# Second layer's dense pass: four normalisations issued one at a time, one per projection, in place of one block

## The reference

```python
    x = _layernorm(x + _L0_attn_ref(x, ...), axis=-1)
    x = _layernorm(x + _L0_ffn_ref(x, ...), axis=-1)      # the norm that the change moves
    x = _layernorm(x + _L1_attn_ref(x, ...), axis=-1)     # its q, k, v projections are the dense pass
    x = _layernorm(x + _L1_ffn_ref(x, ...), axis=-1)

    def _L1_attn_ref(x, q_w, q_b, kv_w, kv_b, o_w):
        q = (x @ q_w.T + q_b) * scale
        kv = x @ kv_w.T + kv_b
        k, v = (kv[..., :E], kv[..., E:])
        q = _rope(q)
        k = _rope(k)
        ...
```

## Time and profile before

| what | us |
|---|---|
| median of 3 runs | 2558.74 |
| lowest and highest of them | 2558.12, 2559.43 |
| the profiled execution, its own time | 2556.79 |
| its span (first to last instruction) | 2555.0 |
| dense pass: start of the stage to the first `qk` | 1250 to 1307.35 |
| first `qk` matmul of chunks 0, 1, 2, 3 | 1307.35, 1377.04, 1448.21, 1517.54 |

### The profile page before, as it was taken

One profiled execution on the slowest core, in us unless ns is written; L12 is line 12 of the kernel. 1 busy time (PEld: TensorE's weight loads), 2 busy tenths in 40 slices (PEclk: granted clock), 3 DMA queues, 4 the chain that ended last, 5 costly groups with the idle time before them and its releaser, 6 DMA issues. The chain is left out here.

```text
span 2555.0 us, 28187 instructions
## 1 busy us (share of the span) xinstructions
PE 2264.4 (89%) x10204; PEld 1546.1 (61%) x10204; DVE 1230.9 (48%) x2284; ACT 748.4 (29%) x1344; POOL 595.8 (23%) x398
## 2 busy tenths in 40 slices
PE   7977899999997899999656777999997899999997
PEld 5854555554543544444344555888886787878875
DVE  6764667776633532222254443222222755555556
ACT  2322555555563321111122222111211421212222
POOL 4232455655553140000022211000000211120200
PEclk9976999999998899999878888999999899999999
DMA  4463444333202341222323325211112201010101
GB/s 178 171 178 96 121 108 116 96 85 78 51 18 99 125 189 46 83 74 83 126 95 107 116 98 203 70 41 46 45 41 73 77 17 33 9 41 0 33 17 50
DMA packets 111936, 212.89 MB, mean 83 GB/s; under 512 B 11008, under 2 KB 28672, under 8 KB 110528
## 3 DMA queue, kind: packets, MB, share of 16 engines
q1 hardware_dynamic: 102720, 181.26, 22.9%
q0 software_dynamic: 8240, 27.01, 3.0%
q10 hardware_dynamic: 864, 3.15, 0.3%
HBM read 136.27 MB, written 75.10 MB: 83 GB/s over the span
## 5 line engine op out<-in xcount | busy, mean ns | idle before, releaser
L619 ACT ACTIVATE a_probs<-a_stb 128x512 f32<-128x512 f32 (+3 forms) x640 | 309.3, 535 | 284.1 <-PE a_stb L731 168.0
L590 POOL TENSOR_TENSOR a_probs<-a_probs 128x1024 f32<-128x1024 f32 (+3 forms) x160 | 281.9, 1774 | 290.1 <-PE a_avb L743 274.2
L645 DVE TENSOR_REDUCE a_mparts<-a_sbank 128x1 f32<-128x512 f32 x384 | 239.6, 682 | 101.4 <-PE a_sbank L705 101.1
L56 PE MATMUL m_gu<-hi,m_wh 128*128 128x512 f32 x512 | 202.9, 396 | 15.6 <-DVE m_h L2046 14.2
L1978 POOL CAST m_wh<-m_wst 128x1024 fp32r<-128x1024 f32 x24 | 28.1, 1170 | 784.0 <-DMA m_wst<-in_w_mlp 425.0
L57 PE MATMUL m_gu<-lo,m_wh 128*128 128x512 f32 x512 | 201.6, 394 | 0.0
L58 PE MATMUL m_gu<-hi,m_wl 128*128 128x512 f32 x512 | 201.5, 394 | 0.0
L705 PE MATMUL a_sbank<-hi,q 96*128 96x512 f32 (+3 forms) x320 | 136.1, 455 | 23.8 <-PEq L152 11.9
L743 PE MATMUL a_avb<-a_probs,V 128*32 128x512 f32 (+3 forms) x1280 | 155.9, 560 | 0.7 <-ACT a_probs L619 0.7
L650 DVE CUSTOM_DVE_ANT_0 a_junk<-a_sbank,hidden 128x128 bf16<-128x128 f32 (+3 forms) x256 | 113.6, 487 | 82.9 <-PE a_sbank L705 81.3
L2046 DVE TENSOR_TENSOR m_h<-m_sg,m_gu 128x512 f32<-128x512 f32 x64 | 43.9, 686 | 193.4 <-ACT m_sg L2008 193.3
(11 more groups left out here) (248 smaller groups left out, 4780.2 us busy)
## 6 DMA issues: line engine op xcount, KB each, us to landing
qk<-v_hl SPq DMA_DIRECT2D x32, 512.0 KB, 2.9
hi<-qk SPq DMA_DIRECT2D x60, 256.0 KB, 4.8
lo<-qk SPq DMA_DIRECT2D x60, 256.0 KB, 5.5
q<-qk SPq DMA_DIRECT2D x48, 256.0 KB, 5.7
m_wst<-in_w_mlp SPq DMA_DIRECT2D x24, 512.0 KB, 3.3
xs<-a_zeros POOLq DMA_DIRECT2D x39, 256.0 KB, 2.5
V<-xs SPq DMA_DIRECT2D x39, 256.0 KB, 2.8
ys<-e_rows_b SPq DMA_DIRECT2D x39, 256.0 KB, 2.0
```

Source lines behind the costliest of these rows:

```text
L56: nc.tensor.matmul(out, wh, xh, start=start, stop=False, skip_group_check=True)
L590: nc.gpsimd.tensor_tensor(probs[:, i % PSLOTS, hs, w0:], probs[:, i % PSLOTS, hs, w0:], probs[:, (i + 1) % PSLOTS, hs, w0:], ALU.add)\
L619: nc.scalar.activation(probs[:, i % PSLOTS, h, w0:], stb[:, k % 3, w0:], ACT.Exp, scale=SCALE0)\
L645: nc.vector.reduce_max(to, sbank[:, b, :], AX).then_inc(s["unit_max"], 1)
```

## The change

`norm` becomes an event for one tile. In a chunk with `more`, `norm 0` stays behind `qk 0`, and `norm 1`, `norm 2` and `norm 3` go behind `rotary 0`, `rotary 1` and `rotary 2`. Ahead of the first chunk the four stay together, but each now runs from its additions to its write before the next begins.

```diff
-                  [("weight", i, 0) for i in range(2 * ND, 3 * ND)] + [("norm", 0, 0)] +
+                  [("weight", i, 0) for i in range(2 * ND, 3 * ND)] + [("norm", t, 0) for t in range(TC)] +
...
-            ev = [("qk", 0, 0)] + [("norm", 0, 1)] * more + [("qk", 1, 0), ("rotary", 0, 0), ("qk", 2, 0)]
-            ev += [("rotary", 1, 0), ("qk", 3, 0), ("rotary", 2, 0), ("v", 0, 0), ("rotary", 3, 0)]
+            ev = [("qk", 0, 0)] + [("norm", 0, 1)] * more + [("qk", 1, 0), ("rotary", 0, 0)]
+            ev += [("norm", 1, 1)] * more + [("qk", 2, 0), ("rotary", 1, 0)] + [("norm", 2, 1)] * more
+            ev += [("qk", 3, 0), ("rotary", 2, 0)] + [("norm", 3, 1)] * more + [("v", 0, 0), ("rotary", 3, 0)]
...
-                        if n > 0:
+                        if n > 0 and j == 0:
                             pool.wait_ge(s["xstore"], 16 * n * TC)
                             pool.wait_ge(s["xt_ok"], n * TC)
-                        for t in range(TC):
-                            k = n * TC + t
-                            nc.gpsimd.indirect_dma_start(
-                                xn[:, t, :], None, ys_dram[:, :],
-                                bass.IndirectOffsetOnAxis(ap=slot_a[:, k:k + 1], axis=0)).then_inc(s[f"routed_a{t}"], 16)
...
+                        k = n * TC + j
+                        nc.gpsimd.indirect_dma_start(
+                            xn[:, j, :], None, ys_dram[:, :],
+                            bass.IndirectOffsetOnAxis(ap=slot_a[:, k:k + 1], axis=0)).then_inc(s[f"routed_a{j}"], 16)
...
-                        for t in range(TC):
-                            nrm.root(act, t, (c + ahead) * TC + t)
+                        nrm.root(act, j, (c + ahead) * TC + j)
...
-                        for t in range(TC):
-                            nrm.apply(dve, xn[:, t, :], rows[t], t, n * TC + t)
+                        nrm.apply(dve, xn[:, j, :], row, j, n * TC + j)
```

More of the change, by code:

```diff
@@ L1415, in run @@
                     elif what == "norm":
-                        for t in range(TC):
-                            nrm.wait(sp, (c + ahead) * TC + t + 1)
-                            sp.dma_start(x2[bass.ds((c + ahead) * CH + t * P, P), :], xn[:, t, :])\
-                                .then_inc(s["xstore"], 16)
+                        nrm.wait(sp, (c + ahead) * TC + j + 1)
+                        sp.dma_start(x2[bass.ds((c + ahead) * CH + j * P, P), :], xn[:, j, :])\
+                            .then_inc(s["xstore"], 16)
                     elif what == "rotary":
@@ L1444, in run @@
                         n = c + ahead
-                        if n > 0:
+                        if n > 0 and j == 0:
                             pool.wait_ge(s["xstore"], 16 * n * TC)
                             pool.wait_ge(s["xt_ok"], n * TC)
-                        for t in range(TC):
-                            k = n * TC + t
-                            nc.gpsimd.indirect_dma_start(
-                                xn[:, t, :], None, ys_dram[:, :],
-                                bass.IndirectOffsetOnAxis(ap=slot_a[:, k:k + 1], axis=0)).then_inc(s[f"routed_a{t}"], 16)
[L1453 to L1457, removed]
+                        k = n * TC + j
+                        nc.gpsimd.indirect_dma_start(
+                            xn[:, j, :], None, ys_dram[:, :],
+                            bass.IndirectOffsetOnAxis(ap=slot_a[:, k:k + 1], axis=0)).then_inc(s[f"routed_a{j}"], 16)
+                        if k >= 2:
+                            pool.wait_ge(s["add_b"], k - 1)
+                        nc.gpsimd.indirect_dma_start(
+                            routed[:, j % 2, :], None, ys_dram[:, :],
+                            bass.IndirectOffsetOnAxis(ap=slot_b[:, k:k + 1], axis=0)).then_inc(s[f"routed_b{j % 2}"], 16)
                     elif what == "qk":
@@ L1545, in run @@
                         n = c + ahead
[L1546 to L1555, removed]
+                        row = X[:, bass.ds(n * TC + j, 1), :].rearrange("p o n -> p (o n)")
+                        dve.wait_ge(s[f"routed_a{j}"], 16 * (n + 1))
+                        nc.vector.tensor_tensor(row, row, xn[:, j, :], ALU.add).then_inc(s["add_a"], 1)
+                        dve.wait_ge(s["add_a"], n * TC + j + 1)
+                        dve.wait_ge(s[f"routed_b{j % 2}"], 16 * (n * (TC // 2) + j // 2 + 1))
+                        nc.vector.tensor_tensor(row, row, routed[:, j % 2, :], ALU.add).then_inc(s["add_b"], 1)
+                        wait_alone(dve, s["add_b"], n * TC + j + 1, s["add_b"], 1)
+                        nrm.mean_and_var(dve, row, j, n * TC + j)
                         if ahead:
```

## The result

| | median, us | lowest to highest | runs |
|---|---|---|---|
| before | 2558.43 | 2555.48 to 2559.43 | 4 |
| changed | 2604.60 | 2600.41 to 2608.09 | 4 |

The changed kernel is slower: ratio 1.0182, 95% interval 1.0162 to 1.0202. Its profiled execution took 2601.93 us.

What follows compares the result with a forecast made beforehand. It took DVE's path from first cosine product to the bias addition of `v 1` to set each chunk, lengthened by a ring paying every gather's lag. 43.7 + 1.8 = 45.5 us gave 2604 us, range 2594 to 2617.

Steps and rivals of the forecast that it cites:

- nine rounds of 15.34 and their surroundings: Chunks 0 to 2: three rounds each plus the stretches around them make 63.24 us a chunk, +43.7 us in all.
- the ring: Chunks 0 to 2: dependence loop through POOL, transfer, DVE, ACT, DVE and back to POOL, once per tile, 15.34 us.
- The round: One pass from a cosine product to the next: 2.55, 3.47, 2.99, 0.54, 0.65 and 5.14, together 15.34 us.
- the 0 to 3.6 us for the stores in the gathers' way: Query stores' landing may overlap gathers by 0.4 us, nine times; unknown cost, taken as 0.
- each chunk's own tail: From the bias addition of `v 1` to the next chunk's first matmul, 12.86 us in chunk 0, claimed unchanged.
- Ahead of chunk 0: Each of four tiles shows 0.54 us round by ACT instead of 0.10: 4 x 0.44 = +1.8 us.
- PE's waits: In the chunks: 12.4 us wait shrinks to about 3.5, new ones of some 6, near 10 before `v 2`.
- Clock and stores at nothing: TensorE's clock and the query stores beside the gathers, both unknown costs in the chunks, each taken as 0.
- a bound of 13 and 3.6: Upper limits in us: 13 if slow matmuls take 0.245 more each on the path, 3.6 for the stores.
- The rival of a low clock (2621): All 36 path matmuls of each chunk at 1.2 GHz, plus stores: 2621 us; chance 0.07 for above 2617.
- The first rival: Interleaving works if gathers are in time: rounds of 9.32 us, 2550 us; needs lag 1.2 us; chance 0.02.
- Its 2523 us for PE's three waits: Case within the faster rival: all three 12.4 us PE waits in the chunks vanish with nothing replacing them, 2523 us.

Runs made afterwards that it cites:

- gathers_one_ahead: Changed kernel, but POOL issues gathers of tiles 0 and 1 behind the first product, tile 2 behind the second, tile 3 behind the third: 2562.57 us, ratio 1.0016.
- product_after_adds: gathers_one_ahead plus a POOL wait: products of `qk 1` to `qk 3` start after both additions of the tile ahead of them on DVE: 2548.99 us, ratio 0.9961.
- roots_behind_qk1: Kernel before, with the four roots on ACT alone moved behind the copies of `qk 1`: 2555.04 us, ratio 0.9984.
- norm_ahead_of_qk0: Kernel before, with the whole block of four normalisations ahead of `qk 0`, ACT's roots staying behind `qk 0`: 2517.92 us, ratio 0.9847.
- gathers_in_block: Changed kernel, but POOL issues all eight gathers of the next chunk behind the first product, as before: 2560.67 us, ratio 1.0009.

## Why the prediction was right

The forecast of 2604 us met the median of 2604.6. By its steps, for the three chunks (nine rounds of 15.34 and their surroundings gave +43.7; +46.66 came):

- The mechanism is the one forecast: the ring over POOL's product, the gather, DVE, ACT and DVE is in the rows, and its parts have the forecast's lengths.
- The round: 140.06 us for nine (46.92, 46.55 and 46.59 a chunk), 15.56 each, +2.0 in all. In the round shown, product to issue 2.53 (2.55 predicted), issue to first addition 3.40 (3.47), to the aggregate 3.18 (2.99; the second gather is waited for 0.89 us), to the reciprocal 0.64 (0.54), to the sine product 0.66 (0.65), to the next product 5.14 (5.14). Issue to first addition is 3.36 to 3.64 in the 12 tiles, so the 0 to 3.6 us for the stores in the gathers' way were rightly taken as 0. The two that were short are the second gather's wait and the root's way by ACT: aggregate to reciprocal is 0.64 or 0.65 in all 12 tiles of the chunks, 0.1 longer than in the first layer's row. Why that is stays open.
- Start of a chunk to its first product: 26.2 for the three, 25.8 before. Last product to the next chunk: 90.57 us for the three where the prediction's terms, with each chunk's own tail, make 90.04. These two are the remaining 0.95.
- Ahead of chunk 0: +1.92 against +1.8. Aggregate to reciprocal is 0.54 to 0.55 there, where it was 0.10 to the next instruction.
- PE's waits: 3.83 us where about 3.5 was said, 6.51 and 4.92 where 6 was said. In front of `v 2` the prediction said near 10; it is 6.99. That wait carried no term of the sum.
- Clock and stores at nothing: PEclk was 0.81 to 0.84 and became 0.78 to 0.80. The sum left 2.95 us over for everything that was costed at nothing, of a bound of 13 and 3.6, and the rows above place two thirds of that in the rounds. The slower matmuls lie beside the ring: the stretch with `qk 0` and the one with `v 3`, where they would be on the path, grew by 0.95 us together. The rival of a low clock (2621) did not come. Its bound was too high: 0.245 us a matmul is the difference of two lengths, but matmuls overlap. Start to start they stand 0.43 us apart where the granted clock is 0.50 and 0.23 where it is 1.00 (1308 to 1311 and 1312 to 1317 in the kernel before), 0.20 a matmul, which makes 11 us and not 13. And PE is idle for about a third of the three chunks, not for half of each round.
- The total agreed more closely than its parts: the sum was 3 us short in the stage, the stage began 4.4 us earlier in the profiled execution, and that execution lay 2.7 us under its median. The hit to within 1 us is luck. What is not luck is the stage itself: 45.5 us forecast, 48.6 measured, with each term near its own value.
- The first rival's mechanism needed a gather lag under 1.2 us a round. gathers_one_ahead and product_after_adds show what the change is worth when the gathers are in time: nothing as long as the addition and POOL's product collide, 9.4 us when they are kept apart. Its 2523 us for PE's three waits fell with roots_behind_qk1.

The Trainium skill, "DMA: Bandwidth & Descriptors", section "Anatomy of one DMA — SWDGE (gpsimd) path", would make the lag 2.6 us and the total about 2596, an estimate. By that figure, the trace does not agree: issue to use is 3.37 and 3.40 us with DVE waiting (1316.74 to 1320.11, 1332.21 to 1335.61), issue to landing is 3.4 us in the median of these gathers, and the measured total is 8.6 us above that sum. Plain transfers of the same 256 KB that POOL issues in the same trace (`xs<-a_zeros`) land after 2.4 us, so it is these gathers by row index that take longer, not all that POOL issues.

The Trainium skill, "Perfetto Trace Analysis", section "Optimization Strategy", says that interleaving may help where the busiest engine changes. By that rule, the runs agree only after the gathers go ahead and DVE and POOL are kept apart (-9.4 us); as written the interleaving cost 46 us. The same section advises to make the dependences of a gap start sooner. By that advice, norm_ahead_of_qk0 agrees: its three chunks took 39.9 us less.

## What to carry to other kernels

When a block that begins with a transfer is cut up and spread among other steps, look at where its issue lands in the issuing engine's queue: if it falls behind an instruction that waits for the previous step, the pieces form a ring, and every piece pays the transfer's whole lag (here 6 us of product and lag, nine more times). Add up the ring from its rows before anything else; a wait of the busiest engine says little of the gain by itself (37.2 us of waits gave 3 to 5). And before a block is interleaved, try it whole and earlier, where its lag and its work fall into idle time of the engine that does it.

## What was not expected of the hardware

DVE and POOL held each other up. In gathers_one_ahead a 128x512 addition of two tiles took 2.77 us in place of 0.69 while POOL's product ran, and the product itself took 2.72 in place of 2.39, having begun inside the addition ahead of that (1331.43 to 1332.12). In gathers_in_block the write of the normalised tile (L802) took 2.16 us in place of 0.55 against a product at 1332.67, and ended 0.3 us behind it:

```profile
1332.67 2.38 POOL L1465 TENSOR_TENSOR q_t<-q_qkf,q_cs 128x1024 f32<-128x1024 f32 x1
```

```profile
1332.35 0.18 DVE L791 BATCH_NORM_AGGREGATE norm_mv<-norm_stats 128x2 f32<-128x6 f32 x1
1332.99 0.16 DVE L800 RECIPROCAL norm_rstd<-norm_std 128x1 f32<-128x1 f32 x1 [0.46 <-issue]
1333.19 2.16 DVE L802 TENSOR_SCALAR q_xn<-X,norm_mv,norm_rstd 128x512 f32<-128x512 f32 x1
```

The reciprocal, in the midst of the same product, kept its 0.16 us. It was there to be seen before: L1600 took 1.78 us at 1357.46 beside a product at 1356.30, where its usual time is 0.69 (kernel before, POOL and DVE):

```profile
1356.30 2.39 POOL L1465 TENSOR_TENSOR q_t<-q_qkf,q_cs 128x1024 f32<-128x1024 f32 x1 [4.84 <-DVE lo L1584]
```

```profile
1357.46 1.78 DVE L1600 TENSOR_TENSOR q_vhl<-q_t,q_vhl 128x512 fp32r<-128x512 f32 x1 [0.70 <-ACT q_vhl L1522]
```

The Trainium skill, "SBUF — State Buffer", section "SBUF: two separate sides", has DVE and GpSimd share a pair of ports that one of them holds for a whole instruction, asked for by DVE operations with two inputs in SBUF or in a mode that uses both ports. By that rule, the trace agrees for the additions, which stand until POOL's product is over. The reciprocal, a small operation with one input, goes through. That the write of the normalised tile runs in such a mode no run here shows; it is held like the additions.
